# Expert networks of a graph network on one core: the outputs of the last two slots reach their nodes by a 0/1 matrix on TensorE, and the gathers of the others begin with the store of slot 14

## The reference, cut to what matters

```
x1 = layer 0: relational graph convolution, random-feature attention, then experts (768 -> 192 -> 384 -> 768)
x2 = layer 1: attention mixer, two graph attention convolutions, then experts (768 -> 1152 -> 768)

experts:  s = xn @ Wg + bg                       # 625 x 8, xn = normalised x
          for each node the two best experts e0, e1, with gates g0, g1
          y = x + g0 * mlp[e0](xn) + g1 * mlp[e1](xn)    # plus the output biases
```

## Time and profile before

| | us |
|---|---|
| median of 3 runs | 2325.12 |
| runs | 2324.09, 2325.67, 2325.12 |
| the profiled execution's own time | 2330.68 |
| its span in the trace | 2329.0 |
| PE busy | 2101.0 (90%) |
| DVE busy | 1424.1 (61%) |
| ACT busy | 922.5 (40%) |
| POOL busy | 396.5 (17%) |

### The profile page before, as it was taken

The page is one execution under the profiler, slowest core; times in us unless marked ns, Lnnn a source line. Parts: engine busy times, 40 slices in busy tenths (PEclk is TensorE's granted clock), DMA queues, the critical chain, the costliest instruction groups (busy, mean ns, idle before and its releaser), DMA issues. The chain is left out here.

```text
span 2329.0 us, 32237 instructions
## 1 busy us (share of the span) xinstructions
PE 2101.0 (90%) x12766; PEld 2021.2 (87%) x12766; DVE 1424.1 (61%) x2283; ACT 922.5 (40%) x1220; POOL 396.5 (17%) x216
## 2 busy tenths in 40 slices
PE   6999999999999999999869949788889968999994
PEld 5898999998999999999849949687789947999994
DVE  7655555565763233333469874358984777888885
ACT  2342255554441111111137723125522225777772
POOL 1674200000302444443010022210000020000001
PEclk9999999999999999999969979999999978999997
DMA  6222233333340111110159951110122037999995
GB/s 221 42 49 63 89 116 131 119 117 138 114 143 21 61 41 58 45 62 1 55 207 336 298 213 62 48 46 28 64 61 90 1 151 278 374 367 374 375 369 185
DMA packets 158239, 326.89 MB, mean 140 GB/s; under 512 B 14376, under 2 KB 99336, under 8 KB 158090
## 3 DMA queue, kind: packets, MB, share of 16 engines
q1 hardware_dynamic: 133354, 265.66, 32.7%
q10 hardware_dynamic: 18976, 43.31, 5.2%
q0 software_dynamic: 5760, 15.86, 2.2%
HBM read 278.22 MB, written 46.49 MB: 139 GB/s over the span
## 5 line engine op out<-in xcount | busy, mean ns | idle before, releaser
L659 PE MATMUL banks<-weight_hi,xt_hi 128*128 128x384 f32 (+2 forms) x2208 | 738.1, 334 | 45.2 <-DVE xt_lo L1436 14.3
L662 PE MATMUL banks<-weight_lo,xt_hi 128*128 128x384 f32 (+2 forms) x2208 | 722.9, 327 | 0.0
L663 PE MATMUL banks<-weight_hi,xt_lo 128*128 128x384 f32 (+2 forms) x2208 | 722.5, 327 | 0.0
L659 PEld LDWEIGHTS banks<-weight_hi,xt_hi 128*128 128x128 f32 x2208 | 423.0, 192 | 57.0 <-issue 28.1
L662 PEld LDWEIGHTS banks<-weight_lo,xt_hi 128*128 128x128 f32 x2208 | 422.8, 191 | 0.4 <-issue 0.2
L663 PEld LDWEIGHTS banks<-weight_hi,xt_lo 128*128 128x128 f32 x2208 | 422.1, 191 | 0.0
L1902 DVE TENSOR_TENSOR weight_lo<-weight_raw,weight_hi 128x2304 fp32r<-128x2304 f32 (+2 forms) x153 | 340.8, 2241 | 56.7 <-ACT weight_hi L1164 56.4
L1164 ACT ACTIVATE weight_hi<-weight_raw 128x2304 fp32r<-128x2304 f32 (+2 forms) x153 | 286.8, 1882 | 98.2 <-PE banks L659 41.9
L862 POOL TENSOR_TENSOR weight_hi<-weight_raw,columns 128x2304 fp32r<-128x2304 f32 x20 | 80.5, 4028 | 691.7 <-DMA weight_raw<-L_gnn_root_in 322.4
L1664 DVE TENSOR_TENSOR held_lo<-banks,held_hi 128x384 fp32r<-128x384 f32 x80 | 44.6, 558 | 213.1 <-ACT held_hi L1090 213.1
L2522 PE MATMUL banks<-held_hi,a_rel 128*128 128x384 f32 (+1 forms) x550 | 171.5, 340 | 2.8 <-ACT a_rel L1105 2.8
(11 more groups left out here) (404 smaller groups left out, 3492.1 us busy)
## 6 DMA issues: line engine op xcount, KB each, us to landing
weight_raw<-L_ffn_w_in SPq DMA_DIRECT2D x102, 1152.0 KB, 7.5
weight_raw<-L_gnn_W_in SPq DMA_DIRECT2D x32, 1152.0 KB, 5.5
weight_raw<-L_ffn_W_in SPq DMA_DIRECT2D x17, 1152.0 KB, 11.4
products<-bias_rows SPq DMA_DIRECT2D x80, 192.0 KB, 1.9
slot_in<-slot_rows ACTq DMA_DIRECT2D x34, 384.0 KB, 5.9
slot_out<-bias_rows ACTq DMA_DIRECT2D x34, 384.0 KB, 7.2
weight_raw<-L_ffn_W_in SPq DMA_DIRECT2D x17, 576.0 KB, 9.9
product_back<-products SPq DMA_DIRECT2D x10, 960.0 KB, 4.6
```

Of the source, the lines that this page charges most:

```text
L659: ins = pe.matmul(dst, s[0], m[0], start=start, stop=False)
L662: pe.matmul(dst, s[0], m[1], start=False, stop=False)
L663: return pe.matmul(dst, s[1], m[0], start=False, stop=stop)
```

## The change

It gives the last two slots, 15 and 16 (`LATE` = 2, `LATE_FROM` = 15), another way back. They are not stored. DVE makes, in turns 11 to 15, a matrix of zeros and ones for each tile and each of the two slots (128 slot rows by 128 nodes, `late_cols`), out of copies of all places and gates that every partition holds (`choice_all`, 1280 places and 1280 gates each). Those copies are written to DRAM by ACT ahead of turn -2 or -1 and in turn 3 and read back, broadcast to 128 partitions, in turn 5. In turn 6 DVE limits the places for the gathers (`place_main`) and puts the gates of late pairs to zero; in turns 7 to 10 it picks out, row by row, the gates of the late slots (`late_gate`). ACT and DVE multiply the outputs of slots 15 and 16 by these gates when they split them (`late_y`). PE multiplies matrix and outputs (`late_products`, 8 products of 128x384 per tile), and DVE adds the result to the node (`late_sums`). POOL's gathers begin when slots 0 to 14 are stored, and DVE does `expert_sums` of tiles 0, 1 (layer 0) or of all tiles (layer 1) ahead of `output(16)`; tile 2's follows it in layer 0. The gathers go to other buffers (`out_rows`), so the tiles from 2 on wait for weight buffers (`LAST_RAW`).

In layer 0 the first mixer piece is also loaded earlier (`LAST_RAW0`), and the split of the second one moves behind `end_phase`, into the loop over the tiles.

The core of the diff:

```diff
+LATE = 2
+LATE_FROM = XSLOTS - LATE
+LATE_ROW = LATE_FROM * SLOT_ROWS
+PLACES = TILES * CHOSEN * P // 4
...
-        out_rows = [[V, XN1], [x[:, :, :].rearrange("p k c -> p (k c)").bitcast(F32).rearrange("p (t d) -> p t d", t=TILES) for x in XT]]
+        free = slice(2 * P, COLS)
+        choice_all = [x[:, 0:4, 2 * P:2 * P + PLACES] for x in XT_place]
+        late_row, late_gate = first_at[:, 0:LATE], is_more[:, 0:LATE]
...
+        out_rows = [x[:, :] for x in slot_in] + y_rows + [r[:, i * DIM:(i + 1) * DIM] for r in raw_more for i in range(3)]
...
 SP
-            sp.wait_ge(e_lo[0], RAWS + SPLITS[0])
+            sp.wait_ge(e_lo[0], RAWS + LAST_RAW0 + 1)
...
+                    if c == 1:
+                        sp.wait_ge(e_lo[0], RAWS + SPLITS[0])
...
 POOL
                 for b in range(2):
-                    pool.wait_ge(y_out[n][b], 16 * len(range(b, XSLOTS, 2)))
+                    pool.wait_ge(y_out[n][b], 16 * len(range(b, LATE_FROM, 2)))
+                pool.wait_ge(placed, 3 * (n + 1))
                 for t in range(TILES):
+                    if t == 2:
+                        pool.wait_ge(e_lo[n], RAWS + LAST_RAW[n] + 1)
...
 ACT
                 def rows_out(v):
+                    if v >= LATE_FROM:
+                        s = v - LATE_FROM
+                        act.wait_ge(late_hot, TILES * LATE * (n + 1))
+                        for c, (bank, _, width) in enumerate(full_cols(n, last)):
+                            act.wait_ge(y_full[n], 2 * v + c + 1)
+                            act.activation(late_y[s][0][:, c, :], ps[:, bank, 0:width], ACT.Copy, scale=late_gate[:, s:s + 1]).then_inc(late_hi, 1)
+                        return
...
+                act.dma_start(choice_dram[0], place_f[:, :]).then_inc(choice_moved, 16)
                 for turn in turns(n):
+                    if turn == 3:
+                        act.wait_ge(comb_ready, 2 * (n + 1))
+                        act.dma_start(choice_dram[1], gate[:, :, :].rearrange("p t k -> p (t k)")).then_inc(choice_moved, 16)
+                    if turn == 5:
+                        act.wait_ge(choice_moved, 64 * n + 32)
+                        for into, src in zip(choice_all, choice_dram):
+                            act.dma_start(into, src.rearrange("p j -> (p j)").partition_broadcast(P).rearrange("p (c n) -> p c n", c=4)).then_inc(choice_moved, 16)
...
+                if n == 0:
+                    act.wait_ge(e_used[0], LAST_RAW0 + 1)
+                    unit_hi(U_MIX1)
+                    act.activation(warm[:, LN_IN1:LN_IN1 + 1], eps_col[:, :], ACT.Sqrt)
                 rows_out(XSLOTS - 1)
-                if n == 0:
-                    act.wait_ge(e_used[0], SPLITS[0])
-                    for c in range(2):
-                        unit_hi(U_MIX1 + c)
...
 DVE
+                def late_step(turn):
+                    if turn == 6:
+                        vec.wait_ge(masks, 2 + 4 * (n + 1))
+                        vec.tensor_scalar(place_main, place_f[:, :], float(LATE_ROW - 1), None, ALU.min).then_inc(placed, 1)
+                        vec.wait_ge(choice_moved, 64 * n + 32)
+                        flat = gate[:, :, :].rearrange("p t k -> p (t k)")
+                        order.step(vec.scalar_tensor_tensor(flat, place_f[:, :], float(LATE_ROW), flat, ALU.is_lt, ALU.mult))
+                        vec.wait_ge(choice_moved, 64 * (n + 1))
+                    if 7 <= turn < 7 + 2 * LATE:
+                        s, i = (turn - 7) // 2, (turn - 7) % 2
...
+                        order.step(vec.scalar_tensor_tensor(choice_kept, choice_all[0][:, one_half], late_row[:, s:s + 1], choice_all[1][:, one_half],
+                                                            ALU.is_equal, ALU.mult, accum_out=sums[i]))
...
+                    if 11 <= turn < 11 + TILES:
...
+                        for s in range(LATE):
+                            order.step(vec.tensor_scalar(into[s], at_tile[:, 0], late_row[:, s:s + 1], None, ALU.is_equal))
+                        order.wait()
+                        for s in range(LATE):
+                            vec.scalar_tensor_tensor(into[s], at_tile[:, 1], late_row[:, s:s + 1], f32(into[s]), ALU.is_equal, ALU.add).then_inc(late_hot, 1)
...
+                if n == 0:
+                    unit_lo(U_MIX1)
+                for t in range(TILES if n == 1 else 2):
+                    expert_sums(n, t)
                 output(XSLOTS - 1)
                 if n == 0:
-                    for c in range(2):
-                        unit_lo(U_MIX1 + c)
+                    expert_sums(0, 2)
...
             for t in range(TILES):
-                expert_sums(0, t)
+                if t < 3:
+                    late_sums(0, t)
+                if t in (2, 3):
+                    expert_sums(0, t + 1)
+                    late_sums(0, t + 1)
...
 PE
+            def late_products(n, t):
...
+                for c in range(2):
+                    for s in range(LATE):
+                        for half in range(2):
+                            ins = pe.matmul(ps[:, bank + c, 0:WCOL], late_cols(s, t), late_y[s][half][:, c, :], start=s + half == 0, stop=s + half == LATE)
+                ins.then_inc(y_full[n], 1)
             experts(0)
             end_phase(pe, "pe", 3)
+            for t in range(3):
+                late_products(0, t)
...
+                    if start == PR_Q and t < 2:
+                        late_products(0, t + 3)
```

More of the change, by code:

```diff
@@ L148, in build @@
         slot_rows_dram = dram("slot_rows", (XSLOTS * SLOT_ROWS, DIM), F32)
-        slot_out_dram = [dram(f"slot_out{n}", (XSLOTS * SLOT_ROWS, DIM), F32) for n in range(2)]
+        slot_out_dram = [dram(f"slot_out{n}", (LATE_ROW, DIM), F32) for n in range(2)]
+        choice_dram = [dram(f"choice_{name}", (P, CHOICES), F32) for name in ("places", "gates")]
         count_dram = dram("counts", (P, TILES * COLS), U16)
@@ L166, in build @@
                 back_rows.append(one(f"product_back{k}", [P, TILES, WCOL], F32))
+        with ExitStack() as here:
+            one, pair = allocator(here)
+            XT_place = [one(f"xt_place{k}", [P, KD, COLS], F32) for k in range(2)]
         XT = keep2("xt", [P, KD, COLS])
@@ L928, in expert_rows @@
                 pool.wait_ge(cleared, 16)
-                pool.wait_ge(placed, 2 * (n + 1))
+                pool.wait_ge(placed, 3 * n + 2)
                 for t in range(TILES):
@@ L1203, in experts @@
                             transposed_hi(l, v)
+                    if turn > LATE_FROM:
+                        rows_out(turn - 1)
                     for i, (l, v) in enumerate(visits(n, turn)):
@@ L1211, in experts @@
                             high()
-                        if i == 0 and turn > 0:
+                        if i == 0 and 0 < turn <= LATE_FROM:
                             rows_out(turn - 1)
@@ L1919, in output @@
                         vec.wait_ge(y_full[n], 2 * v + c + 1)
                         vec.tensor_copy(y_rows[v % 2][:, cols], ps[:, bank, 0:width]).then_inc(y_used[n], 1)
+                def late_step(turn):
[8 more added lines that the diff above has]
+                        s, i = (turn - 7) // 2, (turn - 7) % 2
+                        sums = late_gate[:, s:s + 1], total[:, s:s + 1]
+                        one_half = slice(2 * i, 2 * i + 2)
+                        order.step(vec.scalar_tensor_tensor(choice_kept, choice_all[0][:, one_half], late_row[:, s:s + 1], choice_all[1][:, one_half],
+                                                            ALU.is_equal, ALU.mult, accum_out=sums[i]))
+                        order.wait()
+                        if i == 1:
+                            order.step(vec.tensor_tensor(sums[0], sums[0], sums[1], ALU.add))
+                            order.wait()
+                    if 11 <= turn < 11 + TILES:
+                        t = turn - 11
+                        at_tile = choice_all[0].rearrange("p c (n t k) -> p t k c n", t=TILES, k=CHOSEN)[:, t]
+                        into = [late_cols(s, t).rearrange("p (c n) -> p c n", c=4) for s in range(LATE)]
+                        for s in range(LATE):
+                            order.step(vec.tensor_scalar(into[s], at_tile[:, 0], late_row[:, s:s + 1], None, ALU.is_equal))
+                        order.wait()
+                        for s in range(LATE):
+                            vec.scalar_tensor_tensor(into[s], at_tile[:, 1], late_row[:, s:s + 1], f32(into[s]), ALU.is_equal, ALU.add).then_inc(late_hot, 1)
@@ L1928, in experts @@
                             transposed_lo(l, v)
+                    late_step(turn)
                     if turn > 0:
@@ L1954, in expert_sums, with late_sums @@
                 for k in range(CHOSEN):
[L1955 to L1960 removed]
+                    order.step(vec.scalar_tensor_tensor(X[rows, t, :], out_rows[t * CHOSEN + k][rows, :], gate[rows, t, k:k + 1], X[rows, t, :], ALU.mult, ALU.add))
+                    order.wait()
```

(19 more changed lines are left out.)

74 lines of the change are left out of this document (45 added, 29 removed).

## The result

The change makes the kernel slower: 2342.19 us, median of four runs (2338.54 to 2345.28), against 2324.65 before; the ratio is 1.0063, 95% interval 1.0046 to 1.0081. Forecast were 2324.1 and a range from 2314 to 2332. The profiled execution took 2345.28, its span is 2343.6, against 2330.68 and 2329.0. The medians lie 17.5 us apart, the two traces 14.6, and these 14.6 us are what the traces can be asked for.

A forecast was written before the change was run, and what follows sets the result against it. The last 40 us were bound by slot 16's store, ten gathers and two sums, layer 1's turns by PE, part of layer 0 by transfers. 6.3 + 2.5 + 0.3 - 10.1 = -1.0 us gave 2324.1, range 2314 to 2332.

The forecast's parts named there:

- Layer 1, its turns: Layer 1's expert turns: broadcast and DVE's added work just fit into the free time, +0.3 us, ends 0 and +4.
- 5.8 us for a late piece: Layer 1's turns: time left from three weight pieces, 10.5 us, less 2.13 and 2.56 for a piece's two halves.
- Layer 0's turns: Layer 0's expert turns: 3.9 us for the broadcasts' transfers and 2.4 for DVE's added work, +6.3 in all.
- Between layer 0 and the mixer: From layer 0's experts through the mixer's first transposes: start 1.9 us earlier, loop longer, +2.5, ends -2 and +6.
- The end of layer 1: Kernel's end: gathers start 20 us earlier, 40 PE products follow DVE's sums; gain 10.1 us, ends 8 and 12.
- A: Whole kernel: what the end gains, layer 0 gives back; 2320.5 to 2329 us, chance 0.42.
- B: Whole kernel clearly faster: layer 0's transfers catch up during half clock, mixer's start costs nothing; 2317.4 us, chance 0.36.
- C: Layer 0's turns 6 to 12: DVE's extra time and late weights meet, PE idles; +6.8, 2331.9 us, chance 0.19.
- D: End of layer 1: gathers come no earlier, the end gains nothing; +9.1, 2334.2 us, chance 0.03.
- DVE waiting for gathers at the end: End of layer 1: named as showing the prediction wrong; DVE's ten sums were to run back to back.

The follow-up runs named there:

- the late place: Kernel before plus only DVE's extra forms, results unused, just ahead of each turn's last lower half of a weight piece: 1.0020, layer 1's turns 294.09.
- the late path in layer 1 alone: The change with its new way back for slots 15 and 16 only in layer 1, layer 0 and mixer start as before: 1.0014, layer 1's turns 299.77.
- the change with 88 products: The whole change plus 88 unused 128x128 products on PE behind layer 0's experts: 1.0028, layer 1's turns 301.12.
- Forms alone: Kernel before plus only DVE's extra instructions of turns 7 to 15, results unused, ahead of the weight halves: 1.0039, layer 1's turns 297.96.
- the early broadcast: New way back in layer 1 only, DVE's forms ahead of the last lower half, broadcasts issued in turn 0 instead of 5: 0.9981, turns 294.65.

## Why the prediction was wrong

**Layer 1, its turns: the step that failed.** The prediction left 5.8 us for a late piece, took 2.5 off for late transfers, let the broadcast's 3.2 just fit into the rest and DVE's 1.0 into its free 2.9, and so had +0.3, with ends 0 and +4. Measured: +13.9. Three errors are in it.

- *DVE's free time was counted, not placed.* 2.9 us free per turn said nothing of where: the forms stood ahead of lower halves that free the next load's buffer. At that place they cost 3.9 in layer 1, at the late place 0.0. (They also took 1.37 per turn in place of 1.0.)
- *Room for one delay was taken for room for all.* The broadcast's 3.2 was sized well (3.4 measured) but paid in full: in a ring whose loads are already waited for (37.8 us of ACT's waits before) the delay was not worked off in these runs. The two together cost 5.7 (the late path in layer 1 alone) to 7.0 in this layer (the change with 88 products).
- *Not on the list at all:* the other 7. The change's products in layer 0 shift PE's code, and with it the instruction fetch of every turn of layer 1. The code alone took one kernel to 301.30, from 294.65 to 298.35, and the other from 308.01 back to 301.12. The prediction priced the added products by their time on PE and has no term for their code, which puts it at nothing without a reason.

**Layer 0's turns**, forecast +6.3. Three traces with this code of layer 0 took 125.4, 126.8 and 128.7 to PE's last expert product, mean 127.0 against 122.5: +4.5. Forms alone cost 2.2 and 3.2 by one trace each (2.4 forecast), the broadcasts 1.9 with one pair and 6.7 with two (3.9 forecast for a pair). Traces with the old layer 0 differ by 6.1 among themselves, so the term is right as far as single traces tell, and they can't tell whether 3.9 was. By the Trainium skill (DMA: Bandwidth & Descriptors, Anatomy of one DMA), which gives the moving part of a transfer as bytes over 436 GB/s, an estimate for the broadcasts is 3.0; in layer 1, 3.2 go by the 408 GB/s of that stretch, and 3.4 were measured.

**Between layer 0 and the mixer**, forecast +2.5: +4.2 in this trace, and +1.2 in the mean of the six kernels with this order and no added products (47.6 to 53.5, against 49.5). In the change's trace the first products for the nodes start at half clock, as priced, behind a wait of 12.32, but at 1368.04; the gathers landed 3.16 later than DVE came for them. Two additions of the prediction are off, without effect: the end's 2305.3 + 9.0 is 2314.3 (it has 2314.4), and 1363.7 + 2.6 + 1.0 + 3.6 is 1370.9 (it has 1371.1).

**The end of layer 1**, forecast -10.1 with ends 8 and 12: -7.5 in the change, because its weights and so its gathers were late; -9.4 (19.19 against 28.62) where the turns were as before, with the first gather 5.0 behind slot 14's store, PE's wait 5.70 and 40 products in 9.0, near what was worked out. The term was right and hung on one that was not.

**Rivals.** A had the place of the loss wrong. B, clearly faster, is out: the mixer's start did cost, and layer 0 grew. C, slower, had the direction and the wrong reason: in it layer 0's turns compound and grow by more than 12, which they did not, and layer 1 has only 1 us. D is out: the first gather stands 16.8 ahead of PE's last expert product, before 3.6 behind it. One sign of being wrong that the prediction named, DVE waiting for gathers at the end, was met, by 1.67 and 1.08.

**Left open:** how one fetch delays loads; whether the early broadcast helps (299.2 to 294.7, 296.9 or 298.4 where the fetch is at 11 us, with ratios whose intervals overlap, and 308.0 to 307.7 where it is at 3 to 5); and the +4.8 us of the forms at the late place, of which layer 0's 3.2 come from one trace.

## What to carry to other kernels

Where buffers are freed, loaded, rounded and freed again in a ring, ask of added work not whether the engine has time but what stands behind it in that ring; just ahead of an instruction that waits anyway it cost layer 1 nothing here. A transfer added to a stretch whose loads are already waited for cost about its whole length (3.4 us for 1.31 MB), so price it so. And compare kernels whose code lengths differ with care: the same stage can differ by 7 us in 2325 because code ahead of it moved.

## What the runs showed of the hardware that I had not expected

- With 40 more products ahead of it and nothing else changed, an instruction fetch of 16 KB per turn of 21.05 us stood 3 to 5 us behind a slot's store in place of 11 to 12; the first four stores took 7.4 to 8.8 us in place of 6.0 to 6.7, and fourteen turns were 3 to 7 us longer. The 80 instructions moved it by 7.6 us of 21.05 (the mean over the first four stores), which makes them about 5.8 KB (an estimate from those numbers).
- `slot_out1` at another DRAM address: no difference that can be told (0.9991, interval 0.9975 to 1.0006).
- Ahead of the last products PE's clock stayed up over a wait of 1.45 us and fell over waits of 5.70 and 6.70, with 3.9 and 5.8 us of work at half clock behind them. About 2 us went either way: before, it was down behind one of 2.00, and in the change it stayed at 1.00 over one of 2.03 (2298.43).
